# A decoder layer on one core: key weights' low halves in two pieces, half the last weight load behind two gathers, and expert tile 0 ahead of the last rows

## The chip, the cores and the metric

One Trainium2 chip, one core. The metric is the device time of one execution in microseconds (us); the median of several executions is compared.

## What is computed

`x` is 16 sequences of 128 tokens with 256 channels; `ctx` has the same shape. Cut to what matters, the reference is:

```
x = x + softmax(causal(rope(LN(x) Wq) . rope(LN(x) Wk) / 16)) (LN(x) Wv)
q, k, v = LN(x) Wq' + bq, ctx Wk' + bk, ctx Wv' + bv        8 heads of 128
x = x + concat(softmax(q . k over a dilated window of 64) v) Wc^T + bc
t = LN(x);  logits = silu(t rw1 + rb1) rw2 + rb2             8 experts, the best 2 of each token
x = x + t + sum over the 2 experts  w_e * (silu(t ew1_e + eb1_e) ew2_e + eb2_e)
```

LN is a layer norm over the channels. Matrices are 256x256 for the first attention, 1024x256 for each projection of the second, 256x512 and 512x256 for each expert.

## The kernel before, in words

**Numbers in two halves.** A float32 operand is held as a float16 "high" part and a float16 "low" remainder, and a product is three matmuls (high.high, high.low, low.high; the helper `three`, L1507 to L1512). ScalarE (ACT) writes high parts, VectorE (DVE) the low parts with a two-source instruction (value times a scale, minus the high part).

**Stages.** The 16 sequences go in four groups of 4 (512 tokens). For each group `front` does the first attention and the key and value projections of the second, `back` the queries, the window attention and the output projection. The first `front(0)` (called with r=None) also turns the weights into halves. `back(g)` and `front(g+1)` are in a hardware loop, the last ones stand outside it. After `back(3)` comes the expert stage: 39 tiles of 128 rows, 17 of which (`FULL`) can be filled from the first three groups; each tile is gathered from DRAM by an indirect DMA of GpSimd (POOL, `gather`), turned on TensorE (PE) (`turn`, L1680), copied by ACT (`take`, L744), put through its expert's two layers (`first_layer` L1868, `second_layer` L1882), weighted by DVE (`weigh_out`) and scattered. PE's loop over tiles (L1907) holds the second layer three tiles behind the first. The last group's layer norm, router and expert choice are done among the first tiles of that stage, in two halves of two sequences (`last_rows`, `last_turned`, `last_hidden`, `last_logits`, then `choose` and `weigh` on DVE).

**Order.** Each engine runs its own list in the order in which it is written; semaphores tie the lists together. There is no planner.

**The opening (`front(0)`).** On PE (L1581 to L1631): two products for rope's query halves, two for its key halves (all into the banks `pj0` and `pj1`), the values of the first attention into `ov` and `op`, then `project(g, 0, range(4))`, the first four of eight key products of the second attention, into `pj0` and `pj1` again; then the first attention's scores (L1611, L1616), which wait for both rope additions (`rope_add` 2) and for the masks (`ready` 2); then key products 4 to 7. Before the key products PE waits once for the key weights' low half (`w2_lo` 1, L1602). On DVE (L958 to L1000): the first rope pair (four multiplications, L967 and L968), then the context's low half (L822), the key weights' low half as one instruction of 128x2048 (L844), two casts (`identb` L975 and `masks` L976), then the second rope pair, which waits for POOL's first rope addition (`rope_add`, L963) because it overwrites `rope`; then the value weights' low half (L844 again). On POOL (L454 to L471 and L491 to L493): an addition and a subtraction for each rope pair (L461, L462), and ahead of the first a wait for the DMA that brings the bias row `bcs` (L492).

**Between `back(3)` and the tiles.** SP issues the load of all second-layer weights, four pieces of 1 MB one after the other (L413, L414), when the last scores are done. POOL: gathers 0 and 1, the last layer norm's power for half 0, gather 2, power for half 1, gather 3 and on (L519 to L530); gather 3 reuses the slot of tile 0, so it waits for ACT's `take(0)` and DVE's `take(0)` (which reads the tile's gate). ACT: high part of the last rows' half 0, `take(0)`, `take(1)`, `last_turned(0)`, and in the loop's first pass the high part of half 1, `take(2)`, `last_hidden(0)` (L766 to L783). DVE: low part of half 0, the residual of sequence 3, targets, a small low part, layer norm statistics of half 1, `last_turned(0)`, `take(0)`, `take(1)`, layer norm of half 1 (L1390 to L1437). PE: `turn(0)`, `turn(1)`, `last_rows(0)`, then tile 0's first layer, `turn(2)`, `last_hidden(0)`, tile 1's first layer (L1897 to L1941).

Of the kernel before, what the change touches and what calls it, by code (L numbers as in the profile page):

```python
# [16 lines left out]
P = 128  # L17
# [83 lines left out]
def decoder(nc, a, out):  # L101
# [9 lines left out]
    with ExitStack() as ctx:  # L111
# [221 lines left out]
        def _(sp):  # L333
# [77 lines left out]
            sp.wait_ge(sc_full[0], SC[0] * (G - 1) + 5)  # L411
            sp.wait_ge(sc_full[1], SC[1] * (G - 1) + 4)
            for i in range(4):  # L413
                sp.dma_start(down[:, 2 * i:2 * i + 2], split[:, 2 * i:2 * i + 2]).then_inc(split_in, 16)  # L414
            sp.wait_ge(b2_lo, 1)
            sp.dma_start(b2[E:2 * E, :], b2l[0:E, :]).then_inc(b2_lo_in, 16)
# [27 lines left out]
        def _(pool):  # L444
# [44 lines left out]
                            .then_inc(norm2, 1)  # L489

            power(1, 0)  # L491
            pool.wait_ge(bc_in, 16)  # L492
            front(0)  # L493
            with pool.Fori(0, G - 1) as g:
                back(g, True)
# [3 lines left out]
            def gather(t):  # L499
                s = t % SLOTS  # L500
                if t >= SLOTS:
                    pool.wait_ge(tp_free, t - SLOTS + 1)
                    pool.wait_ge(gated, t - SLOTS + 1)
                known = B if t >= FULL else OLD
                pool.indirect_dma_start(got[s], None, rows[0:known * L],  # L505
                                        bass.IndirectOffsetOnAxis(src_row[:, t:t + 1], 0),
                                        bounds_check=known * L - 1, oob_is_err=False).then_inc(gathered[s], 16)
# [14 lines left out]
            gather(1)  # L522
            power(3, G - 1, HALVES[0])
            gather(2)
            power(3, G, HALVES[1])
            for t in range(SLOTS, TILES):
                if t == FULL:
                    pool.wait_ge(row_out, 16 * G + 16)
                    pool.wait_ge(idx_done, 2)
                gather(t)  # L530
                if t >= TRAIL:
                    scatter(t - TRAIL)
                if t == CHOOSE + 5:
                    pool.wait_ge(gdiff, G)
                    pool.tensor_tensor(ge[:], euler[:], gd[:], ALU.pow).then_inc(gexp, 1)
                if t == NEW_LANES + 5:
                    pool.wait_ge(hot_t_done, 1)
                    pool.tensor_tensor(pay.rearrange("p (j t) -> p j t", j=JO + JN),
                                       hot_t.rearrange("p (j t) -> p j t", j=JO + JN),
                                       signed.unsqueeze(2).to_broadcast([P, JO + JN, REST]), ALU.mult).then_inc(pay_done, 1)  # L540
# [4 lines left out]
        def _(act):  # L545
# [183 lines left out]
            def last_high(h):  # L729
                high(3, G - 1 + h, row[:, HALVES[h], 0:D], HALVES[h])  # L730
# [33 lines left out]
                act.activation(hTh[t % SLOTS][:], hT[k][:], ACT.Copy, scale=MID).then_inc(h_hi, 1)  # L764

            act.wait_ge(row_out, 16 * (G - 1) + 16)  # L766
            last_high(0)
            take(0)
            take(1)
            last_turned(0)  # L770
            for t in range(TILES + 1):
# [20 lines left out]
        def _(dve):  # L792
# [46 lines left out]
                dve.wait_ge(tpB_full, TPB * g + 1)  # L839
                dve.tensor_copy(xTl[:], tpB[:].bitcast(F16)).then_inc(tpB_free, 1)  # L840

            def weights_low2(i, src):
                dve.wait_ge(w2_hi, i + 1)
                dve.scalar_tensor_tensor(out=w2l[:, :, 1024 * i:1024 * i + 1024], in0=src, scalar=UP,  # L844
                                         in1=w2h[:, :, 1024 * i:1024 * i + 1024], op0=ALU.mult,
                                         op1=ALU.subtract).then_inc(w2_lo, 1)

            def part_low(r, k):
                dve.wait_ge(part_hi, 4 * r + k + 1)
# [108 lines left out]
            def front(g, r=None, final=False):  # L958
                cosb = cosT.unsqueeze(1).to_broadcast([P, GB, P])
                sinb = sinT.unsqueeze(1).to_broadcast([P, GB, P])  # L960
                for i in range(2):
                    if r is not None or i:
                        dve.wait_ge(rope_add, 2 * g + i)  # L963
                    for half in range(2):
                        dve.wait_ge(pj_full[half], PJ * g + i + 1)
                        src = pj[half][:].rearrange("p (b t) -> p b t", b=GB)
                        dve.tensor_tensor(rope[:, 3 * half].rearrange("p (b t) -> p b t", b=GB), src, cosb, ALU.mult)  # L967
                        last = dve.tensor_tensor(rope[:, 1 + half].rearrange("p (b t) -> p b t", b=GB),  # L968
                                                 src, sinb, ALU.mult)
                        last.then_inc(pj_free[half], 1)  # L970
                    if i == 0:
                        if r is None:
                            context_low(0)
                            weights_low2(0, wkf)
                            dve.tensor_copy(identb[:], ident)  # L975
                            dve.tensor_copy(masks[:], cst[:, 2 * P:7 * P].rearrange("p (m k) -> p m k", m=5))\  # L976
                                .then_inc(ready, 1)
                        else:
                            norm(3, r, x2)
                if r is None:  # L980
                    weights_low2(1, wvf)
                else:
                    rows_low(r)
# [302 lines left out]
            def back(g, more):  # L1286
# [87 lines left out]
                if not more:  # L1374
                    sums(7)
                    transposed(6)
                    outputs_low(4)
                    sources(TABLE_OLD, FULL, 0)
                    outputs_low(5)
                    residual(1, op)  # L1380
                    transposed(7)
                    outputs_low(6)
                    tile_experts(full_first, full_n, FULL, 0)
                    outputs_low(7)
                    dve.wait_ge(op_free, OP * g + 2 + 2)
                    norm(3, G - 1, x2, HALVES[0])
                    residual(2, op)
                    pack(0, WORDS_FULL)
                    weights_low()
                    normed(3, G - 1, x2, HALVES[0])  # L1390
                    rows_low_half(0)
                    residual(3, sc1)
                    targets(FULL, 0)
                    dve.wait_ge(b2_hi, 1)
                    dve.scalar_tensor_tensor(out=b2l[0:E, :], in0=b2f[0:E, :], scalar=UP, in1=b2[0:E, :], op0=ALU.mult,
                                             op1=ALU.subtract).then_inc(b2_lo, 1)
# [35 lines left out]
            norm(3, G, x2, HALVES[1])  # L1432
            dve.sem_inc(y_free, 1)
            last_turned(0)
            take(0)
            take(1)
            normed(3, G, x2, HALVES[1])  # L1437
            for t in range(TILES + LAG + 1):
# [55 lines left out]
        def _(pe):  # L1494
# [86 lines left out]
            def front(g, r=None):  # L1581
# [31 lines left out]
                for b in range(GB):  # L1613
                    s = slice(b * P, (b + 1) * P)
                    for c in range(KC):
                        last = pe.matmul(sc0[:, s], qr[:, c, s], kr[:, c, s], start=False,  # L1616
                                         stop=(c == KC - 1), skip_group_check=True)
                last.then_inc(sc_full[0], 1)
                project(g, 0, range(4, 8))
                if r is not None:  # L1620
                    turn_rows(r, SC[0] * r + 6, SC[1] * r + 4)
# [4 lines left out]
                last.then_inc(tpA_full, 1)  # L1626
                if r is None:
                    pe.wait_ge(w2_hi, 2)
                    pe.wait_ge(w2_lo, 2)
                project(g, 1, range(1))  # L1630
                pe.wait_ge(tpA_free, TPA * g + 2)  # L1631
                for i, (bank_, full, free, use) in enumerate(first):
# [172 lines left out]
            pe.wait_ge(w1_lo, 1)  # L1805
            front(0)
            pe.wait_ge(w2_hi, 3)
            pe.wait_ge(w2_lo, 3)
            with pe.Fori(0, G - 1) as g:
                back(g, True)  # L1810
                front(g + 1, g)
# [88 lines left out]
            pe.wait_ge(packed_done, 1)  # L1900
            load(0)
            words = [experts()]
            last_rows(0)
            pe.wait_ge(up_lo, 1)
            pe.wait_ge(spare_lo, 3)
            pe.wait_ge(split_up_in, 16)
            for t in range(TILES + LAG):  # L1907
                k = column(t) % STEPS
                if t == 0:
                    pe.wait_ge(op_free, OP * G - 1)  # L1910
                if t == 1:
                    pe.wait_ge(op_free, OP * G)
                    pe.wait_ge(sc_free[1], SC[1] * (G - 1) + 4)
                if t < TILES:
                    first_layer(t, words[-1][k])
                then = None
                if t + 1 < TILES:
                    if column(t + 1) % STEPS == 0:
                        words.append(experts())
                    then = words[-1][column(t + 1) % STEPS]  # L1920
                if t < LAG and then is not None:
                    for m in range(MC):
                        addresses(then, m)
                if t == LAG:
                    pe.wait_ge(split_in, 64)
                    pe.wait_ge(b2_lo_in, 16)
                if t >= LAG:
                    old = column(t - LAG)
                    second_layer(t - LAG, words[old // STEPS][old % STEPS], then)
                if k == LOAD_AT and column(t) // STEPS + 1 < WORDS and t < TILES:  # L1930
                    if column(t) // STEPS + 1 == WORDS_FULL:
                        pe.wait_ge(packed_done, 2)
                    load(column(t) // STEPS + 1)
                if t + 2 < TILES:
                    turn(t + 2)
                if t == 0:
                    last_hidden(0)
                if t == 1:
                    last_rows(1)
                if t == 2:  # L1940
                    last_hidden(1)  # L1941
                if t == 3:
                    last_logits()
                if t == NEW_COUNTS:
                    ranks(slice(OLD, B), 2, LOGITS)
                if t == NEW_LANES + 3:
                    table(JO + JN, REST, 2, JO // 8 + 1, RANK_NEW)
# [94 lines left out]
```

## Time and profile before

| what | value |
|---|---|
| median of 3 runs | 481.01 us (480.35 to 483.81) |
| the profiled execution's own time | 480.62 us |
| its span in the trace | 478.8 us |
| time around the span | 1.82 us |
| granted TensorE clock, mean over the span | 0.982 of full |

Times in the rows are counted from the span's start. Engines are PE (TensorE matmul), PEld (its weight load), DVE (VectorE), ACT (ScalarE), POOL (GpSimd), SPq (the queue of the engine that issues DMAs). A row of a timeline is a run of like instructions: start, time, engine, line, operation, what is written and read, how many, and in brackets how long the engine was idle before it and what ended that. Buffers that share memory carry the name of the memory: the key weights' halves are `up_f`, the rope operands `up`, the gathered tiles `cst`.

### The profile page before, as it was taken

The page shows a single profiled execution, that of the slowest core. Times are in us where ns is not written, and L with a number is a line of the kernel's source. Part 1 is how long each engine was busy: PE and PEld are TensorE (multiplying, and loading weights), DVE is VectorE, ACT ScalarE, POOL GpSimd, SP SyncE. Part 2 cuts the span into 40 slices and gives each one's busy share as a digit, 9 for nine tenths or more (in the row PEclk, how much of TensorE's full clock was granted, in tenths as well). Part 3 has the DMA queues.
Part 4 walks back from the last instruction along what each step waited for, and adds up shares of the span by engine and source line. Part 5 has one row for each costly group of instructions (what it writes and reads, how often), then busy time and mean ns, then how long its engine had stood idle before and what let it go on. Part 6 is the DMA issues. An engine that isn't in the chain of part 4 may idle for free.

```text
span 478.8 us, 12291 instructions
## 1 busy us (share of the span) xinstructions
PE 444.6 (93%) x4211; PEld 306.3 (64%) x4211; DVE 346.8 (72%) x859; ACT 276.6 (58%) x716; POOL 165.4 (35%) x168
## 2 busy tenths in 40 slices
PE   8799999999998999999999998888899999999980
PEld 3356468856457865546785644677776788888850
DVE  5945467786876778696679688897678885555577
ACT  4454657526547526555762665573676777777740
POOL 1230123050203213012405020234346777777640
PEclk9989999999999999999999999999899999999995
DMA  8901000134230041621003423618113248223566
GB/s 323 371 40 46 0 2 1 36 99 168 97 133 0 0 131 44 219 88 45 1 15 117 134 86 135 242 54 341 41 46 125 76 139 270 81 81 88 157 230 244
DMA packets 20412, 54.43 MB, mean 114 GB/s; under 512 B 3365, under 2 KB 9774, under 8 KB 19600
## 3 DMA queue, kind: packets, MB, share of 16 engines
q1 hardware_dynamic: 16336, 43.34, 25.5%
q0 software_dynamic: 3744, 9.47, 6.9%
q10 hardware_dynamic: 288, 1.05, 0.6%
q8 instruction: 25, 0.41, 0.4%
q14 instruction: 19, 0.16, 0.1%
HBM read 37.00 MB, written 17.76 MB: 114 GB/s over the span
## 4 chain that ended last, share of the span: by engine, by line
PE 69%; DVE 15%; issue 10%; ACT 2%; POOL 1%; DMA 1%; DVEq 1%; POOLq 0%; ACTq 0%; SPq 0%
PE pj L1511 11%; PE pair L1511 10%; PE op L1788 8%; PE pair L1888 3%; PE tpA L1888 3%; PE sc L1878 3%; PE pj L1878 3%; PE pj L1760 2%; PE op L1878 2%; PE pair L1878 2%; PE sc L1727 2%; PE sc L1687 2%; ACT p L704 2%; PE pair L1890 2%; PE tpA L1890 2%
## 5 line engine op out<-in xcount | busy, mean ns | idle before, releaser
L1511 PE MATMUL pj<-up,up_f 128*128 128x512 f16 x240 | 58.9, 382 | 6.0 <-DVE rope L968 3.5
L704 ACT ACTIVATE p<-sc,nm 128x128 f32<-128x128 f32 (+1 forms) x128 | 41.8, 344 | 33.6 <-DVE nm L1338 33.5
L1511 PE MATMUL pair<-up,up_f 128*128 128x512 f16 x240 | 59.7, 386 | 0.2 <-DVE down L1342 0.2
L505 POOL DMA_INDIRECT cst<-rows,src_row x39 | 48.8, 1251 | 20.4 <-issue 8.0
L516 POOL DMA_INDIRECT picked<-wch,dst_row x39 | 40.1, 1029 | 24.2 <-issue 9.0
L452 POOL TENSOR_TENSOR rstd<-veps,nhalf 128x4 f32<-128x4 f32 (+1 forms) x13 | 12.7, 974 | 103.3 <-DVE veps L804 103.0
L1511 PEld LDWEIGHTS pj<-up,up_f 128*128 128x128 f16 x240 | 22.6, 98 | 34.8 <-issue 3.9
L1511 PEld LDWEIGHTS pair<-up,up_f 128*128 128x128 f16 x240 | 23.5, 99 | 28.8 <-DVE rope L968 1.5
L1788 PE MATMUL op<-wch,outs 128*128 128x256 f16 x240 | 40.3, 273 | 0.0
L487 POOL TENSOR_TENSOR pn<-p,inv 128x256 f32<-128x256 f32 x32 | 18.9, 612 | 44.0 <-DVE inv L1292 44.0
L461 POOL TENSOR_TENSOR up<-rope 128x512 f32<-128x512 f32 x8 | 12.4, 1552 | 60.7 <-DVE rope L968 49.4
L1788 PE MATMUL op<-wcl,outs 128*128 128x256 f16 x120 | 32.7, 273 | 0.0
L546 ACT ACTIVATE up_f<-sc 128x512 f16<-128x512 f16 x39 | 23.2, 594 | 15.6 <-PE sc L1687 15.6
L1888 PE MATMUL tpA<-down,up_f 128*128 x80 | 27.4, 379 | 0.4 <-issue 0.2
L1338 DVE TENSOR_REDUCE nm<-sc 128x4 f32<-128x512 f32 (+1 forms) x32 | 17.8, 555 | 13.4 <-PE sc L1732 7.2
L1888 PE MATMUL pair<-down,up_f 128*128 x76 | 26.2, 379 | 0.9 <-DVE up_f L1260 0.7
L577 ACT ACTIVATE down<-pj,bias 128x512 f32<-128x512 f32 x24 | 16.4, 684 | 18.0 <-PE pj L1511 18.0
L704 ACT ACTIVATION_READ_ACCUMULATOR p<-sc,nm 128x1 f32 x128 | 26.7, 209 | 0.0
L1260 DVE SCALAR_TENSOR_TENSOR up_f<-up_f 128x512 f16<-128x512 f32 x39 | 26.6, 682 | 0.0
L764 ACT ACTIVATE up_f<-up_f 128x512 f16<-128x512 f32 x39 | 24.6, 630 | 1.2
L1788 PEld LDWEIGHTS op<-wch,outs 128*128 128x128 f16 x240 | 22.3, 98 | 3.2
L1511 PE MATMUL pair<-up_f,up 128*128 128x512 f16 x96 | 23.3, 379 | 0.0
(294 smaller groups left out, 1111.3 us busy)
## 6 DMA issues: line engine op xcount, KB each, us to landing
raws<-in_staged SPq DMA_DIRECT2D x12, 512.0 KB, 5.4
split<-halved SPq DMA_DIRECT2D x12, 512.0 KB, 4.0
down<-split SPq DMA_DIRECT2D x4, 1024.0 KB
rows<-row SPq DMA_DIRECT2D x4, 528.0 KB
small<-in_x SPq DMA_DIRECT2D x4, 512.0 KB, 3.7
up<-in_ctx SPq DMA_DIRECT2D x4, 512.0 KB, 4.8
v<-in_w SPq DMA_DIRECT2D x2, 1024.0 KB, 9.2
resid<-outs SPq DMA_DIRECT2D x4, 512.0 KB, 2.8
```

The lines of the kernel that those rows point to most:

```text
L487: pool.tensor_tensor(pn2[:, 0, k], p2[:, 0, k], inv2[:, 0, k].unsqueeze(2).to_broadcast([P, 2, P]), ALU.mult)\
L505: pool.indirect_dma_start(got[s], None, rows[0:known * L], bass.IndirectOffsetOnAxis(src_row[:, t:t + 1], 0), bounds_check=known * L - 1, ...
L516: pool.indirect_dma_start(picked, bass.IndirectOffsetOnAxis(dst_row[:, t:t + 1], 0), ys[s], None, bounds_check=2 * B * L - 1, oob_is_err=F ...
L546: copy = lambda out, in_, scale=1.0: act.activation(out, in_, ACT.Copy, scale=scale)
L704: last = act.activation((p2[:, 0], p2h)[s][:, i, :], logit(s)[:, i, :], ACT.Exp, bias=nm2[:, s, i:i + 1], scale=1.0, accum_out=sum2[:, s, ...
L764: act.activation(hTh[t % SLOTS][:], hT[k][:], ACT.Copy, scale=MID).then_inc(h_hi, 1)
L1260: dve.scalar_tensor_tensor(out=hTl[s][:], in0=hT[t % BANKS][:], scalar=MID, in1=hTh[s][:], op0=ALU.mult, op1=ALU.subtract).then_inc(h_lo, 1)
L1511: last = pe.matmul(out, w(c), v(c), start=(i == 0), stop=(i == len(terms) - 1))
L1788: last = pe.matmul(dst[:, 0:D], o[:, b % 2, h, :], w[:, h, :], start=(h == 0 and k == 0), stop=(h == H - 1 and k == 2))
L1878: ins = pe.matmul(h[:, m * P:(m + 1) * P], up_rows[:, bass.ds(block(e, m, c, w), P)], xt[t % SLOTS][:, x, :], start=(c == 0 and i == 0), s ...
L1888: pe.matmul(y[:], hTh[q][:, m, :], down_rows[:, bass.ds(at, 2 * D)], start=(m == 0), stop=False, skip_group_check=True)
L1890: pe.matmul(y[:, 0:D], hTl[q][:, m, :], down_rows[:, bass.ds(at, D)], start=False, stop=False, skip_group_check=True)
```

## The change

1. The key weights' low half is made by two DVE instructions of 128x1024. The first (columns 0 to 511, key products 0 to 3) stays between the rope pairs; the second, and behind it the two casts, go behind the second rope pair and ahead of the value weights. PE waits for the second piece ahead of key product 4 (`w2_lo` 2), and the later counts of that semaphore go up by one.
2. POOL's wait for the bias row's DMA ahead of the first rope addition is gone. (The bias row is still waited for by DVE at L1026, whose result POOL waits for.)
3. Pieces 2 and 3 of the last weight load are issued only when gather 0 and gather 1 have landed.
4. Gather 3 is issued ahead of the power of half 1.
5. `take(0)` goes ahead of `last_high(0)` on ACT, and on DVE from behind `last_turned(0)` to ahead of the residual of sequence 3. On PE `last_rows(0)` goes behind tile 0's first layer, and `last_hidden(0)` from behind `turn(2)` to behind tile 1's first layer.

```diff
 (SP)
             for i in range(4):
+                if i >= 2:
+                    sp.wait_ge(gathered[i - 2], 16)
                 sp.dma_start(down[:, 2 * i:2 * i + 2], split[:, 2 * i:2 * i + 2]).then_inc(split_in, 16)
 (POOL)
             power(1, 0)
-            pool.wait_ge(bc_in, 16)
             front(0)
...
             power(3, G - 1, HALVES[0])
             gather(2)
+            gather(SLOTS)
             power(3, G, HALVES[1])
-            for t in range(SLOTS, TILES):
+            for t in range(SLOTS + 1, TILES):
 (ACT)
+            take(0)
             last_high(0)
-            take(0)
             take(1)
 (DVE)
-            def weights_low2(i, src):
+            def weights_low2(i, src, cols=slice(0, 1024)):
...
                         if r is None:
                             context_low(0)
-                            weights_low2(0, wkf)
-                            dve.tensor_copy(identb[:], ident)
-                            dve.tensor_copy(masks[:], cst[:, 2 * P:7 * P].rearrange("p (m k) -> p m k", m=5))\
-                                .then_inc(ready, 1)
+                            weights_low2(0, wkf, slice(0, 512))
...
                 if r is None:
+                    weights_low2(0, wkf, slice(512, 1024))
+                    dve.tensor_copy(identb[:], ident)
+                    dve.tensor_copy(masks[:], cst[:, 2 * P:7 * P].rearrange("p (m k) -> p m k", m=5))\
+                        .then_inc(ready, 1)
                     weights_low2(1, wvf)
...
                     rows_low_half(0)
+                    take(0)
                     residual(3, sc1)
...
             last_turned(0)
-            take(0)
             take(1)
 (PE)
                 last.then_inc(sc_full[0], 1)
+                if r is None:
+                    pe.wait_ge(w2_lo, 2)
                 project(g, 0, range(4, 8))
...
-                    pe.wait_ge(w2_lo, 2)
+                    pe.wait_ge(w2_lo, 3)
...
-            pe.wait_ge(w2_lo, 3)
+            pe.wait_ge(w2_lo, 4)
...
-            last_rows(0)
             pe.wait_ge(up_lo, 1)
...
                     first_layer(t, words[-1][k])
+                if t == 0:
+                    last_rows(0)
+                if t == 1:
+                    last_hidden(0)
...
-                if t == 0:
-                    last_hidden(0)
```

## Rows read from the trace of the kernel before

**Rows 1.** The page: busy time of PE and the chain that ended last.

```profile
PE 444.6 (93%) x4211; PEld 306.3 (64%) x4211; DVE 346.8 (72%) x859; ACT 276.6 (58%) x716; POOL 165.4 (35%) x168
...
PE 69%; DVE 15%; issue 10%; ACT 2%; POOL 1%; DMA 1%; DVEq 1%; POOLq 0%; ACTq 0%; SPq 0%
```

**Rows 2.** Timeline of the opening, 16 to 31 us.

```profile
16.10 1.21 DVE L822 SCALAR_TENSOR_TENSOR up<-up 128x1024 f16<-128x1024 f32 x1
...
17.23 2.29 DVE L844 SCALAR_TENSOR_TENSOR up_f<-v,up_f 128x2048 f16<-128x2048 f32 x1
...
18.92 1.47 PE L1511 MATMUL op<-up_f,up 128*128 128x256 f16 x12
18.99 1.65 POOL L461 TENSOR_TENSOR up<-rope 128x512 f32<-128x512 f32 x1 [11.32 <-DMA bcs<-in_bc]
...
19.43 1.29 DVE L975 CAST identb<-dc 128x128 bf16<-128x128 f32 x1
...
20.60 1.26 POOL L462 TENSOR_TENSOR up<-rope 128x512 f32<-128x512 f32 x1
20.65 1.57 DVE L976 CAST masks<-cst 128x640 bf16<-128x640 f32 x1
...
22.13 0.68 DVE L967 TENSOR_TENSOR rope<-pj,cst 128x512 f32<-128x512 f32 x1
...
23.56 1.63 PE L1511 MATMUL pj<-up,up_f 128*128 128x512 f16 x6 [3.16 <-DVE rope L968]
...
24.53 2.28 DVE L844 SCALAR_TENSOR_TENSOR up_f<-v,up_f 128x2048 f16<-128x2048 f32 x1
...
24.75 3.18 POOL L461 TENSOR_TENSOR up<-rope 128x512 f32<-128x512 f32 x1 [2.89 <-DVE rope L968]
24.98 2.77 PE L1511 MATMUL pair<-up,up_f 128*128 128x512 f16 x6
...
29.12 1.46 PE L1511 MATMUL pair<-up,up_f 128*128 128x512 f16 x6
...
30.42 0.38 PE L1611 MATMUL sc<-masks,identb 128*128 128x512 bf16 x1
```

**Rows 3.** POOL's rope addition and DVE's norm in the next group, same timeline.

```profile
99.38 1.27 POOL L461 TENSOR_TENSOR up<-rope 128x512 f32<-128x512 f32 x1 [13.92 <-DVE rope L968]
...
104.59 3.36 DVE L811 TENSOR_SCALAR xn<-outs,mv,rstd_up 128x256 f32<-128x256 f32 x4
```

**Rows 4.** Busy time by stretch: us, PE, PEld, DVE, ACT, POOL busy, clock, DMA share, GB/s.

```profile
20.00:24.00 4.00, 0.84 (x7) 0.34 (x6) 4.00 (x6) 2.40 (x2) 1.86 (x2) 1.00 1.04 393
24.00:28.00 4.00, 4.00 (x13) 1.47 (x12) 2.80 (x3) 0.90 (x2) 3.25 (x2) 0.59 0.28 115
...
40.00:44.00 4.00, 4.00 (x20) 2.20 (x19) 3.27 (x11) 0.88 (x3) 0.00 (x0) 1.00 0.15 23
```

**Rows 5.** DMA issues: the output projection's weights, KB, us from issue to landing.

```profile
down<-in_wc SPq DMA_DIRECT2D x1, 1024.0 KB, 14.8
```

**Rows 6.** Busy time by stretch during the last weight load (columns as in rows 4).

```profile
326.00:328.00 2.00, 1.93 (x45) 1.65 (x44) 1.19 (x3) 1.16 (x3) 1.56 (x2) 1.00 1.00 422
```

**Rows 7.** Timeline from the first gather to the expert choice, 326 to 352 us.

```profile
326.14 1.26 POOL L505 DMA_INDIRECT cst<-rows,src_row  x1 [2.52 <-DVE src_row L1185]
...
333.69 0.41 PE L1687 MATMUL sc<-dc,cst 128*128 128x128 f32 x2 [0.83 <-issue]
...
335.19 0.69 DVE L818 TENSOR_TENSOR row<-xn,row 128x512 f16<-128x512 f32 x1 [1.11 <-ACT row L546]
...
337.30 2.19 PE L1878 MATMUL op<-up_f,up 128*128 128x128 f16 x24
...
339.49 0.15 DVE L1272 TENSOR_SCALAR gate<-cst 128x1 f32 x1 [0.66 <-issue]
...
341.30 0.63 ACT L546 ACTIVATE row<-xn 128x512 f16<-128x512 f32 x1 [3.59 <-DVE xn L811]
...
348.86 0.48 DVE L887 TENSOR_SCALAR rope<-ov,rb1s 128x256 f32<-128x256 f32 x1 [1.99 <-ACT rope L741]
...
351.85 0.32 DVE L917 STREAM_TRANSPOSE logits_t<-ov 128x128 f32<-128x128 f32 x1
```

**Rows 8.** Busy time by stretch between those two (columns as in rows 4).

```profile
341.30:348.80 7.50, 7.01 (x100) 6.47 (x98) 3.80 (x10) 7.44 (x20) 3.72 (x4) 1.00 0.23 64
```

More of the change, by code:

```diff
@@ L840, in turned @@
                 dve.tensor_copy(xTl[:], tpB[:].bitcast(F16)).then_inc(tpB_free, 1)
-            def weights_low2(i, src):
+            def weights_low2(i, src, cols=slice(0, 1024)):
+                at = slice(1024 * i + cols.start, 1024 * i + cols.stop)
                 dve.wait_ge(w2_hi, i + 1)
-                dve.scalar_tensor_tensor(out=w2l[:, :, 1024 * i:1024 * i + 1024], in0=src, scalar=UP,
-                                         in1=w2h[:, :, 1024 * i:1024 * i + 1024], op0=ALU.mult,
-                                         op1=ALU.subtract).then_inc(w2_lo, 1)
+                dve.scalar_tensor_tensor(out=w2l[:, :, at], in0=src[:, :, cols], scalar=UP, in1=w2h[:, :, at],
+                                         op0=ALU.mult, op1=ALU.subtract).then_inc(w2_lo, 1)
             def part_low(r, k):
```

## The prediction

> **What bounds the kernel now.** The page comes first: PE is busy for 93% of the span and holds 69% of the chain that ended last, DVE 15% [rows 1]. So nearly all of the kernel is PE's, and an edit pays only where PE waits, or where it runs at its lower clock. The change touches two such places, and I read the timeline of each. In the opening PE finishes the first attention's values at 20.39 us (18.92 + 1.47) and then stands idle until 23.56, put down to DVE's second rope pair [rows 2]. PE is busy for 0.84 of the 4 us from 20 to 24, and in the 4 us after that its granted clock is 0.59 on average, that is, for most of them the lower level of 1.2 GHz instead of 2.4 [rows 4]. In the second place, after the last output projection, PE is idle for 0.83 us before the first tile is turned, and tile 0's first layer takes 2.19 us; but from 341.3 to 348.8 ACT is busy for 7.44 of 7.50 us [rows 7, 8].
>
> **Opening: when the second rope pair starts.** One fact of these rows must be understood first: POOL and DVE keep each other out. POOL's rope addition takes 1.27 us undisturbed [rows 3], but 3.18 when it starts at 24.75 into DVE's weight instruction, which runs to 26.81; 26.81 + 1.12 is its end [rows 2]. The other way round, the cast of only 128x128 takes 1.29 us beside POOL's first addition, the masks' cast ends 0.36 us behind POOL's second, and four norm instructions take 3.36 us beside two additions [rows 2, 3]. So between 16.1 and 22.2 us these instructions of DVE and POOL are one queue, whose length is a sum. Before, that sum is: context 1.13 (17.23 - 16.10), weights to 19.52, first addition to 20.64, second to 21.86, masks 0.36, and the second rope pair starts at 22.13. The bias row's DMA, on which POOL waits until 18.99, costs less than it looks: DVE holds the weights instruction until 19.52 anyway.
>
> After: POOL may start at 16.2, when the first pair is done, and queues behind the context's instruction, which started first. The sum is 16.10 + 1.13 (context) + 1.13 (a piece of 128x1024, as large as the context's) + 1.22 + 1.26 (POOL's two) = 20.84, in whichever order they take turns. The rope pair starts at 20.9 instead of 22.13. PE's first key product began 1.43 us behind it (23.56 - 22.13, the half of the pair that frees its bank), so it begins at 22.33: **1.23 us gained**, and PE's gap shrinks from 3.2 to 1.9 us.
>
> **Opening: from there to the scores.** Before, the four key products and the wait to the scores took 30.42 - 23.56 = 6.86 us. At full clock a product is spaced 1.30 us (29.12 to 30.42), four are 5.2; the rest is the low clock (the second product's 2.77 against 1.46) [rows 2]. After, two things must be ready. PE: 22.33 + 5.2 = 27.53 if the clock stays up. DVE and POOL: the rope pair ends at 20.9 + 4 x 0.6 = 23.3; the second piece 1.13 to 24.45, POOL's additions 1.22 and 1.26 to 26.95, masks 0.36 to 27.3. The scores start at about 27.6 instead of 30.42: **2.8 us gained**, the 1.23 included. Here late next is PE itself, with the masks 0.3 us ahead of it; the casts moved are hidden only by that much. The value weights' low half then runs from 27.3 to 29.6, and the row maximum that DVE must do when the scores are done (2 us behind their start) at 29.6 is met without loss. The new wait for the second piece (24.45) is over long before key product 4 at 29.6; behind it on PE is everything, but it waits for nothing. Behind this point PE is busy without a gap (4.00 of 4.00 us in the stretch at 40) at full clock [rows 4], and the last of the large weights to be used has landed at 6.62 + 14.8 = 21.4 (its issue at 6.62) [rows 5], so a DMA is not what is late next, and the gain is carried on through the PE-bound groups.
>
> Bounds on the clock: between 0.59 as before, which leaves 22.33 + 6.86 = 29.19, 1.23 us gained, and full clock, 2.8 us. I take full clock, because the gap is 1.3 us shorter and PE is at work from 22.3. The Trainium skill, "TensorE: Matmul & The Clock Gate", Part 1, says that the default is the throttled state, that recent activity releases it, and that the watching is free-running, not tied to the kernel's start; by it the same 1.9 us gap can lose the clock in one execution and not in another, which no row here shows; the sum by it is either of these two.
>
> **The last weight load and the gathers.** The load moves 422 GB/s and fills the DMA engines [rows 6]; gather 0 is issued at 326.14 and its tile is turned only at 333.69, 0.83 us after PE could [rows 7]. After, two 1 MB pieces (2.5 us each at that rate) are through by about 327, gathers 0 and 1 land near 329 to 330.5, and pieces 2 and 3 follow to about 336. They are needed by the second layer of tile 0, near 349: 13 us of cover; if gather 0 landed as late as now, they would end near 340, still covered. On SP the b2 copy stands behind the new waits (it waits for DVE until 337 anyway), and the rows and residual of group 3. Cost 0, gain for PE 0.8 us. Gather 2 moves beside piece 3 and may land 1 us later, at 336.5; its tile is turned near 338.
>
> **PE's new order.** turn(0) at 332.9, turn(1) behind ACT's take(0) at 334.1, tile 0's first layer at 334.9 (337.30 before), at full clock 1.34 us, last_rows(0) to 337.0, about 1 us of address work, turn(2) at 338, tile 1's first layer to 339.5, last_hidden(0) to 340.8. PE is then 2.4 us ahead of before.
>
> **But who waits for that.** DVE's list from 335.19 on is a chain: low part, residual, targets, statistics, last_turned(0), two takes, norm of half 1, ending at 341.27, and ACT's high part of half 1 starts at 341.30 after 3.59 us idle [rows 7]. take(0) is only moved within it (0.66 us of register load and the 0.15 us gate; behind a longer instruction some 0.25 of it may be covered). turn(3) needs ACT's take(2), which stands behind that high part, so PE waits until about 342.4 with most of its lead. From 341.3 ACT is full to 348.8 [rows 8], its tanh then releases DVE at 348.86, and DVE's four steps, a take and hidden_low end at 351.66; the choice of experts starts at 351.85 [rows 7]. That path loses 0.25 us of takes and 0.15 us between hidden_low and the logits: **0.4 us gained**. Bounds: 0 (DVE's register load covered nowhere) and 2.4 (PE's whole lead). POOL's power for half 1 now stands behind gather 3, which waits for take(0) (336.6) and is issued by 337.7; the power is asked for at 338.5 to 339.1, so no cost, but this cover is only 1 us.
>
> **Sum.** 480.62 - 2.8 - 0.4 = 477.4 us against the profiled execution's own time. That one lies 0.39 below the median of 481.01, so medians would be 477.4 to 477.8; I say 477.5.
>
> **Rivals.**
> - The clock falls in the opening again: 480.62 - 1.23 - 0.4 = 479.0. For it: a gap of 1.9 us is still there, and clocks fell behind the 3.2 us gap. Against: PE works right behind it. Chance 0.22.
> - PE's lead counts in the expert stage: if DVE's and ACT's chain from 335 is shorter than I read (take(0) moved frees more, or POOL's earlier gathers do), up to 2.4 us: 480.62 - 2.8 - 2.4 = 475.4. For it: PE is busy 7.01 of 7.50 us in the same stretch [rows 8], nearly a bound itself. Against: ACT's 7.44. Chance 0.16.
> - Slower: gather 0 lands late, and now everything hangs on it: ACT's take(0) stands ahead of the last rows' high part, DVE's ahead of the residual, and SP's last two pieces behind it. Today it has landed by 333.69, 7.5 us after its issue; from about 333.8 on, each us later would be a us of the chain that ends at 341.3. It outweighs the opening's 2.8 from 336.6 on, 10.5 us after issue; at 338 it is 480.62 - 2.8 + 4.2 = 482.0. For it: today's 7.5 us is long. Against: those are explained by 4 MB ahead of it in full DMA engines, and 2 MB go. Chance 0.03.
> - The change does nothing at the opening (the pair waits for something else) and 0.4 in the expert stage: 480.2. Against: the queue's sum ends at 22.2 and the pair starts at 22.13, so nothing else is left for it to wait for [rows 2]. Chance 0.04.
>
> **From the cases to the numbers.** My forecast has 0.55. 1%, 4.8 us, is about what a measurement of this kernel tells from no change; the forecast lies at 0.7%. Faster by over 1%: the second rival's 0.16. Slower by over 1%: 0.02 for things unseen. Within: 0.82. The range reaches from 475.3 (second rival) to 479.6 (first rival with the median's 0.4 and a little).
>
> **What would show it.** In the changed profile: POOL's first addition starts at 16.2 and lasts over 2 us; the second rope pair starts at 20.9; the first key product at 22.3; scores at 27.6; clock 1.00 from 24 to 28; maximum of the scores 2.8 us earlier. In the expert stage relative to PE's end of the output projection: turn(0) without a gap, tile 0's first layer 2.4 us earlier, but ACT's high part of half 1 and the start of the choice only 0 to 0.5 us earlier, and PE idle for over 1 us ahead of turn(3). Wrong would be: a low clock at 24 to 28, the choice 1 us or more earlier, or scores that wait for the masks.

## The result, and the profile after

The changed kernel takes 477.82 us in the median of 8 executions (477.01 to 478.94), the kernel before 481.96 in 8 (480.35 to 483.81). The ratio is 0.9913, with a 95% interval of 0.9889 to 0.9937. The profiled executions are 480.62 and 477.78 us, their spans 478.8 and 475.9. So the time fell by 2.84 us between the two profiled executions (2.9 in their spans) and by 4.1 between the medians, and both numbers have to be explained.

The opening after, in the timeline (it answers to [rows 2]); lines have moved down by 2 to 5, so L824, L847, L463, L464, L981, L982 and L1614 are L822, L844, L461, L462, L975, L976 and L1611 of before:

```profile
16.33 1.22 DVE L824 SCALAR_TENSOR_TENSOR up<-up 128x1024 f16<-128x1024 f32 x1
...
16.56 2.11 POOL L463 TENSOR_TENSOR up<-rope 128x512 f32<-128x512 f32 x1 [8.93 <-DVE rope L970]
17.46 2.29 DVE L847 SCALAR_TENSOR_TENSOR up_f<-v,up_f 128x1024 f16<-128x1024 f32 x1
...
18.63 2.25 POOL L464 TENSOR_TENSOR up<-rope 128x512 f32<-128x512 f32 x1
...
20.91 0.69 DVE L969 TENSOR_TENSOR rope<-pj,cst 128x512 f32<-128x512 f32 x1 [1.16 <-POOL up L464]
...
22.35 1.46 PE L1514 MATMUL pj<-up,up_f 128*128 128x512 f16 x6 [1.72 <-DVE rope L970]
...
25.66 1.57 DVE L982 CAST masks<-cst 128x640 bf16<-128x640 f32 x1
...
27.16 2.28 DVE L847 SCALAR_TENSOR_TENSOR up_f<-v,up_f 128x2048 f16<-128x2048 f32 x1
27.52 0.38 PE L1614 MATMUL sc<-masks,identb 128*128 128x512 bf16 x1
```

Each of POOL's additions and the weights piece of half the size last 2.1 to 2.3 us, nearly twice what they take undisturbed (1.27 us for the addition in [rows 3], 1.22 for the piece in a later run): they take turns. The first addition ends at 18.67, the piece at 19.75, the second addition at 20.88, and the second rope pair starts at 20.91, 1.22 us earlier than before. The first key product starts 1.21 us earlier and the scores 2.90 us earlier. So 1.69 of the 2.90 us come behind the first key product. That the clock is worth all of the 1.69 does not follow; the experiments below put it at 1.2 us in the old order. Against [rows 4] it is 1.00 instead of 0.59 in the stretch from 24 to 28 us (columns as there):

```profile
20.00:24.00 4.00, 2.28 (x14) 1.12 (x13) 3.09 (x5) 2.56 (x3) 1.34 (x2) 1.00 1.03 391
24.00:28.00 4.00, 4.00 (x22) 2.01 (x20) 4.00 (x4) 2.18 (x4) 2.88 (x2) 1.00 0.25 102
```

The place around tile 0, after (it answers to [rows 7]; all times are 2.7 us earlier already when the last output projection ends, at 330.12 instead of 332.85):

```profile
327.66 0.79 SPq L416 DMA_DIRECT2D down<-split  x2
...
329.96 0.38 PE L1692 MATMUL sc<-dc,cst 128*128 128x128 f32 x2
...
332.58 2.57 PE L1883 MATMUL op<-up_f,up 128*128 128x128 f16 x24 [0.71 <-ACT up_f L548]
...
333.54 0.15 DVE L1275 TENSOR_SCALAR gate<-cst 128x1 f32 x1 [0.74 <-issue]
...
338.15 0.63 ACT L548 ACTIVATE row<-xn 128x512 f16<-128x512 f32 x1 [1.94 <-DVE xn L813]
...
339.62 0.84 ACT L743 ACTIVATE rope<-ov,rb1half 128x256 f32<-128x256 f32 x2 [0.35 <-PE ov L1514]
...
342.96 0.41 PE L1692 MATMUL sc<-dc,cst 128*128 128x128 f32 x2 [1.34 <-ACT up_f L548]
...
349.04 0.31 DVE L919 STREAM_TRANSPOSE logits_t<-ov 128x128 f32<-128x128 f32 x1
```

Piece 2 of the weight load is issued at 327.66 and piece 3 right behind it, within the 0.79 us of this row, so gather 0 had landed 4.3 us after its issue at 323.40, and gather 1 by 328.45. Tile 0 is turned without a gap, and its first layer starts 2.46 us behind the output projection instead of 4.45. Yet the choice of experts (the last row) starts 18.92 us behind it instead of 19.00. PE had the lead and lost most of it waiting for ACT, 1.34 us ahead of the turn of tile 4. Of the 2.90 us gained at the scores, 2.73 are left at the end of the last output projection, 2.81 at the choice and 2.9 at the end of the span.

### The profile page after: what moved, and what is told of

Its sections match the earlier page's. It is cut to its first block, busy times and chain, and to the rows that moved or that the text cites. A ratio compares the mean times of both kernels' runs of the same rounds, so it can differ in the third digit from the quotient of the medians.

```text
span 475.9 us, 12293 instructions
## 1 busy us (share of the span) xinstructions
PE 444.0 (93%) x4211; PEld 306.2 (64%) x4211; DVE 348.7 (73%) x860; ACT 277.1 (58%) x716; POOL 166.4 (35%) x168
## 4 chain that ended last, share of the span: by engine, by line
PE 71%; DVE 12%; issue 9%; ACT 3%; POOL 2%; DVEq 1%; ACTq 0%; POOLq 0%
PE pj L1514 12%; PE pair L1514 10%; PE op L1793 8%; PE pair L1893 3%; PE tpA L1893 3%; PE op L1883 3%; PE sc L1883 3%; PE pj L1883 3%; PE pj L1765 2%; PE pair L1883 2%; PE ov L1801 2%; PE sc L1732 2%; PE sc L1692 2%; ACT p L706 2%; PE tpA L1895 2%
## 5 line engine op out<-in xcount | busy, mean ns | idle before, releaser
L1514 PE MATMUL pair<-up,up_f 128*128 128x512 f16 x240 | 58.3, 379 | 0.2 <-DVE down L1345 0.2
L463 POOL TENSOR_TENSOR up<-rope 128x512 f32<-128x512 f32 x8 | 11.8, 1479 | 58.1 <-DVE rope L970 58.1
```

Source lines behind the costliest of these rows:

```text
L1514: last = pe.matmul(out, w(c), v(c), start=(i == 0), stop=(i == len(terms) - 1))
```

## The experiments

Twelve kernels ran, four to a chip. Since the place of an event against the span's start moves by about 1 us between executions (the first rope product starts at 11.96 to 13.05), I compare three distances within each profile: from the first rope product on PE to the scores, from the end of the last output projection to ACT's high part of half 1, and from that same end to the choice of experts. The last column says for how long the clock of the profiled execution was at its lower level around tile 0: short is about 3 us, long about 7. In the opening it fell only in the profile of the kernel before. The mark for the first distance is this row, of the kernel before:

```profile
12.10 1.46 PE L1511 MATMUL pj<-up,up_f 128*128 128x512 f16 x6
```

| kernel | first product to scores | projection to high part | projection to choice | ratio to before (95%) | low clock around tile 0 |
|---|---|---|---|---|---|
| before | 18.32 | 8.45 | 19.00 | 1 | short |
| changed | 15.18 | 8.03 | 18.92 | 0.9913 (0.9889 to 0.9937) | short |
| opening alone | 15.19 | 8.44 | 18.86 | 0.9917 (0.9888 to 0.9946) | short |
| tile 0's parts alone | 17.11 | 8.03 | 18.62 | 0.9975 (0.9956 to 0.9994) | not at all |
| changed, again | 15.19 | 8.03 | 18.88 | 0.9902 (0.9876 to 0.9929) | short |
| bias wait put back | 16.13 | 8.03 | 18.60 | 0.9928 (0.9901 to 0.9955) | not at all |
| bias wait taken away alone | 17.08 | 8.44 | 20.58 | 1.0000 (0.9979 to 1.0021) | long |
| before, PE kept at work | 17.12 | 8.44 | 19.59 | 0.9976 (0.9957 to 0.9995) | long |
| hidden layer back | 15.18 | 8.02 | 18.28 | 0.9903 (0.9870 to 0.9936) | short |
| norm early | 15.19 | 7.21 | 17.98 | 0.9877 (0.9848 to 0.9906) | short |
| old order, PE kept at work | 15.19 | 8.43 | 18.87 | 0.9910 (0.9883 to 0.9936) | not at all |
| norm early, PE kept at work | 15.19 | 7.20 | 17.44 | 0.9880 (0.9854 to 0.9907) | not at all |
| opening alone, again | 15.18 | 8.43 | 19.05 | 0.9914 (0.9885 to 0.9943) | short |
| changed, third time | 15.19 | 8.03 | 18.96 | 0.9903 (0.9874 to 0.9933) | short |

**The two halves, each alone.** The opening alone is the changed kernel with SP's, ACT's, DVE's and PE's lines around tile 0 and gather 3 as before; the other is the reverse.

> Parts 1 and 2 of the change alone (the opening). Theory (the opening carries nearly all): second rope pair at 20.9, scores at 27.5, 2.8 us less than the kernel before, ratio near 0.994; the expert stage as before, shifted. Rival (PE's lead in the expert stage carries half or more): 1.5 us less or under.

> Parts 3, 4 and 5 alone (the last weight load, gather 3, the order around tile 0). Theory: the opening as before; tile 0's first layer 2 us earlier against PE's end of the output projection, the choice of experts 0 to 0.4 us earlier; total 0 to 0.4 us less, ratio 0.999 to 1.000. Rival: 2 us less or more, ratio 0.996.

> The changed kernel itself, beside the other three on one chip: 3 to 4 us less than before; the sum of the two halves if they are independent (opening 2.8, expert stage 0.1 to 0.4).

Measured: 477.66 us (7 executions) for the opening alone, 480.95 (12) for tile 0's parts alone, 477.66 (6) for the changed kernel, 482.26 (18) for the one before. So the opening carries nearly all of it, as the theory said, but the size is 4.6 us and not the 2.8 expected (the interval, 2.6 to 5.4 us, holds both). Tile 0's parts alone took 1.3 us off the median (interval 0.3 to 2.1), more than the 0 to 0.4 expected and less than the rival's 2. The halves do not add up as expected: 4.6 and 1.3 us alone, 4.6 together, where 3 to 4 had been expected. On the profile of tile 0's parts alone something else could be seen. In this execution the clock did not fall in the opening although nothing was changed there, and the scores then waited for POOL's last addition:

```profile
24.00:28.00 4.00, 4.00 (x20) 1.77 (x19) 2.73 (x2) 1.81 (x3) 3.32 (x2) 1.00 0.26 105
```

```profile
29.14 0.39 PE L1614 MATMUL sc<-masks,identb 128*128 128x512 bf16 x1 [0.32 <-POOL up L464]
```

That gives the first distance without a fallen clock, 17.11, and splits the opening's 3.13: 1.21 for the clock in the old order, 1.92 for the order with the clock up. What a fallen clock would cost in the new opening no run shows, since it never fell there.

The same profile shows a price that the staggered weight load has. Gather 2 is issued at 330.71, when pieces 2 and 3 of the load have just gone out (a DMA share of 0.93 from 330 to 332 us and of 1.01 in the 2 us behind), and PE waits for its rows ahead of the turn of tile 2, 6.9 us after that issue:

```profile
337.64 0.41 PE L1690 MATMUL sc<-dc,cst 128*128 128x128 f32 x2 [0.95 <-DMA cst<-rows,src_row]
```

In the changed kernel this gather takes as long (from 329.30 until PE's weight load at 336.19), with only 0.22 us of idle time of PE in front of the turn. The choice of experts is not later for it, at 18.62 us in the profile with PE's wait of 0.95.

**The bias row's wait, put back and taken away alone.**

```diff
 (put back, in the changed kernel)
+            pool.wait_ge(bc_in, 16)
             front(0)
```

```diff
 (taken away alone, in the kernel before)
-            pool.wait_ge(bc_in, 16)
             front(0)
```

> The changed kernel with POOL's wait for the bias row's DMA put back. Theory (DVE and POOL take turns): the first addition starts at 19.0 and is not held up, since DVE has nothing left, the second ends at 21.5, the second rope pair starts at 21.6 instead of 20.9, scores at 28.2: 0.65 us more than the changed kernel if the clock stays up; 1.3 more on top if it falls in the longer gap of PE. Rival (the wait costs what POOL shows as idle): 2.4 us more.

> The kernel before without POOL's wait for the bias row, nothing else. Theory (DVE and POOL take turns, only the sum of their work between the pairs counts): POOL starts at 16.2 but the second rope pair starts at 22.1 as before (16.1 + 1.13 + 2.29 + 1.22 + 1.26 + 0.36 = 22.4), gain 0 to 0.3 us. Rival (POOL's idle time was the cost): rope pair at 20.8 or earlier, 1.2 us less or more.

Put back, the first distance grows by 0.94 (expected 0.65), and the median was 478.59 against 477.66 beside it. POOL's two additions then run undisturbed:

```profile
18.96 1.27 POOL L463 TENSOR_TENSOR up<-rope 128x512 f32<-128x512 f32 x1 [11.43 <-DMA bcs<-in_bc]
20.19 1.26 POOL L464 TENSOR_TENSOR up<-rope 128x512 f32<-128x512 f32 x1
21.48 0.69 DVE L970 TENSOR_TENSOR rope<-pj,cst 128x512 f32<-128x512 f32 x1 [3.17 <-POOL up L464]
```

Taken away alone it brings nothing: POOL starts 2.7 us earlier, and the second rope pair starts at 22.12, against 22.13 in [rows 2]; the ratio is 1.0000. The same work is only queued in another order:

```profile
16.32 2.11 POOL L461 TENSOR_TENSOR up<-rope 128x512 f32<-128x512 f32 x1 [8.70 <-DVE rope L967]
17.23 3.35 DVE L843 SCALAR_TENSOR_TENSOR up_f<-v,up_f 128x2048 f16<-128x2048 f32 x1
...
18.40 3.31 POOL L462 TENSOR_TENSOR up<-rope 128x512 f32<-128x512 f32 x1
...
20.51 1.28 DVE L974 CAST identb<-dc 128x128 bf16<-128x128 f32 x1
21.72 0.48 DVE L975 CAST masks<-cst 128x640 bf16<-128x640 f32 x1
22.12 0.68 DVE L966 TENSOR_TENSOR rope<-pj,cst 128x512 f32<-128x512 f32 x1
```

So the wait was not the cost, and the rival that reads POOL's 11.32 us of idle time as one falls. It is worth 0.94 us only once the weights are in two pieces and the casts are out of the way. This profile also shows what a long fall of the clock can cost: its opening kept the clock, but around tile 0 the clock was at its lower level for about 7 us (twice as long as in the profile of before), and ACT's first tanh waited 1.22 us for the router's hidden layer on PE (in the changed kernel 0.35):

```profile
336.00:338.00 2.00, 2.00 (x23) 1.92 (x22) 1.63 (x7) 0.49 (x1) 0.48 (x1) 0.60 0.01 2
338.00:340.00 2.00, 1.24 (x9) 0.90 (x8) 0.88 (x5) 0.00 (x0) 0.78 (x2) 0.50 0.00 0
340.00:342.00 2.00, 2.00 (x12) 1.43 (x10) 1.09 (x3) 1.11 (x2) 1.54 (x2) 0.50 0.28 76
```

```profile
342.61 0.84 ACT L740 ACTIVATE rope<-ov,rb1half 128x256 f32<-128x256 f32 x2 [1.22 <-PE ov L1510]
```

Its choice of experts starts 20.58 us behind the projection, 1.58 later than in the profile of before, with the same order of work.

**PE kept at work in the old opening.**

```diff
+                    keep_warm(sc1, 14)
                     pe.wait_ge(w2_hi, 1)
```

> The kernel before with 14 matmuls of zeros into an idle bank in PE's gap of the opening. Theory (more than half of the opening's gain is the clock that no longer falls): clock 1.00 from 24 to 28 in every execution, key products at 1.30 us each, scores at 29.15 to 29.3 and then held by POOL's last addition, 1.2 us less than an execution of before in which the clock fell, and none of the high times of before. Rival (the gap alone counts): scores at 30.4 as before.

Measured: 481.08 us against 482.38, ratio 0.9976. The first distance is 17.12, just what the undisturbed opening showed, and the scores again wait for POOL's last addition (0.31 us). So the clock is worth 1.2 of the opening's 3.1 us, where the theory gave it more than half. That the matmuls of zeros are what held the clock in this profile is not shown: two profiles without them, those of tile 0's parts alone and of the bias wait taken away alone, kept it over gaps of 3.16 and 3.14 us. The median speaks for them (interval 0.2 to 2.1 us). The last part of the expectation failed: the executions still reach 482.8, and the profile has the clock low around tile 0 for some 7 us as well, with a distance of 19.59 there. The opening's clock is one thing, tile 0's another.

**Around tile 0: the hidden layer back, the norm early.** In the first, `last_hidden(0)` stands behind `turn(2)` again. In the second also, on DVE:

```diff
                     residual(3, sc1)
+                    dve.wait_ge(op_free, OP * (g + 1))
+                    norm(3, G, x2, HALVES[1])
                     targets(FULL, 0)
+                    last_turned(0)
+                    normed(3, G, x2, HALVES[1])
                     dve.wait_ge(b2_hi, 1)
...
-            norm(3, G, x2, HALVES[1])
             dve.sem_inc(y_free, 1)
-            last_turned(0)
             take(1)
-            normed(3, G, x2, HALVES[1])
```

> The changed kernel with the router's hidden layer of half 0 ahead of tile 1's first layer again, everything else changed. In the changed kernel ACT's first tanh waits 0.35 us for it, since tile 1's first layer stands ahead. Theory: no wait of ACT for PE there, the choice of experts 0.3 us earlier against PE's end of the output projection, total 0.3 us less or even. Rival: PE's order there doesn't matter, choice at the same distance.

> As the run before, and on DVE the norm of half 1 goes ahead of the targets, the small low part and the second take. Theory (DVE's and ACT's chain from the last residual sets the choice of experts): ACT's high part of half 1 starts 0.8 us earlier against PE's end of the output projection than in the changed kernel, the choice 0.8 to 1.1 us earlier, total 0.8 to 1.1 us less than the changed kernel. Rival (PE is the bound there): choice at most 0.3 earlier.

Measured: 476.86 and 476.26 us. In both ACT's first tanh no longer waits for PE. The choice stands 18.28 and 17.98 us behind the projection, 0.64 and 0.94 less than in the changed kernel, and the high part of half 1 in the second 0.82 earlier:

```profile
337.60 0.63 ACT L548 ACTIVATE row<-xn 128x512 f16<-128x512 f32 x1 [1.25 <-DVE xn L813]
338.77 0.84 ACT L743 ACTIVATE rope<-ov,rb1half 128x256 f32<-128x256 f32 x2
```

So DVE's and ACT's chain does set the choice, provided that PE's hidden layer is out of ACT's way; the changed kernel had put it in its way, which costs it something when the clock falls: in the two profiles with the changed order and no fall around tile 0 (tile 0's parts alone, bias wait put back) ACT waits for no hidden layer, and the choice stands at 18.62 and 18.60. Neither of the two kernels ran beside the changed one. Against the kernel before, the first has a ratio of 0.9903, which is that of the changed kernel (0.9902 to 0.9913), so its gain in the distance is not seen in the time; the second has the best ratio of this study, 0.9877, with an interval that reaches over the others.

**PE kept at work around tile 0, and both marks once more.**

```diff
 (4 and 7 in the old order; 0, 4 and 3 with the norm early, which also has 7 in the opening's gap)
+            pe.wait_ge(ov_free, TABLE_OLD)
+            keep_warm(ov, 4)
             turn(0)
+            keep_warm(ov, 7)
             turn(1)
```

> The opening's parts with the old order around tile 0, and 4 + 7 matmuls of zeros around the turn of tile 0. Theory (what the new order adds in the median is that it stands a fallen clock): the clock stays at 1.00 there, the distance from the end of the output projection to the choice of experts is 18.6 us instead of 18.9 to 20.6, the median 0.5 to 1 us below the opening alone and at the changed kernel's. Rival (the new order saves work of PE itself): distance 19 or more, median no better than the opening alone.

> The kernel with the norm of half 1 early, with 7 matmuls of zeros in the opening's gap and 4 + 3 around tile 0's turns. Theory: clock 1.00 in both places in every execution, distance to the choice 17.7 instead of 18.0, median 0.3 us below the same kernel without them (476.3) and 1 to 1.5 us below the changed kernel on this chip. Rival (the filler delays PE's own work): no better than 476.3.

> The opening's parts alone, once more, beside the changed kernel on the same chip: theory says 0 to 1 us above the changed kernel, with single executions 2 to 3 us above its best where the clock falls for long around tile 0. Rival: no difference in median or spread.

> The changed kernel once more, as the mark for the other three: 477 to 478 us, its executions within 2 us of each other.

Measured on one chip: 478.31, 476.50, 478.46 and 477.75 us, before 483.16. The clock did stay up in both filled kernels, 1.00 in every stretch around tile 0. In the old order that brought the distance only to 18.87, not to 18.6, and the median is that of the opening alone: against a short fall of the clock the filler buys nothing (19.05 in the profile of the opening alone beside it). So the expectation failed, and the rival's reading, that the new order also saves a little by itself, is nearer. The changed kernel's median is 0.7 us below that of the opening alone, within what was expected, but its executions spread over 2.8 us instead of the 2 expected, and those of the opening alone over 2.0. The longest of all four kernels is one of the changed kernel, 479.73 us, so long executions are not a mark of the old order. With the norm early the distance fell to 17.44 (expected 17.7), the median to 1.25 us below the changed kernel beside it, as expected; against the same kernel unfilled it can't be told (476.3 on another chip).

## Why the prediction was right, and what it missed

**The two halves, step by step.** These were forecast to the tenth: the second rope pair at 20.9 (20.91) and the first key product at 22.33 (22.35), by adding up what DVE and POOL do between the pairs; and the scores at 27.6 (27.52), with PE itself late next and the masks 0.3 us ahead of it. The start was 0.24 us later in this execution (first rope product at 12.34 instead of 12.10), so measured from there the sum was 0.24 us too cautious: the three turns took 1.12, 1.08 and 1.13 us. The clock was 1.00 from 24 to 28, the end of the bounds that I took. The experiments bear out the sum, but not the split in its bounds: with the clock fallen I had left the change 1.23 us, and so priced the clock at 1.6. In the old order it is worth 1.21, because with the clock up the scores still wait for POOL's last addition, which ends at 29.15; the order is worth 1.92.

**The expert stage.** PE's lead was forecast at 2.4 us and its uselessness too. Tile 0's first layer came 2.0 us earlier against the projection's end, the high part of half 1 0.42 us earlier (forecast 0.25), the choice 0.08 (forecast 0.4). Two steps of that were off. I put the end of PE's hidden layer at 340.8 and thereby ahead of ACT, at "full clock 1.34 us" for tile 0's first layer; it took 2.57 us with the clock falling, and even at 1.00 it takes 2.21 (tile 0's parts alone) and 2.10 (norm early, filled), where the first layer of tile 2 takes 1.50. Tile 0's is the only one whose weight addresses are not worked out ahead of it, which is the likely reason; no run took it away. Then ACT waited 0.35 us for PE. And I expected PE to stand ahead of the turn of tile 3; it stood ahead of that of tile 4. Gather 2 was put 1 us late at most, with its tile turned near 338; against the projection's end the turn came about 1 us later than that.

**The size in the medians.** The sum, 480.62 - 3.2 = 477.4, was made against a profiled execution, and that was one of the shorter ones: the first median of three was 481.01, that of eight 481.96, of the later sets 482.3 to 483.2. So the forecast of 477.5 came close to 477.82, but the gain between the medians, 4.1 us, is larger than the 3.5 forecast. Between the two profiles it is 2.84 against 3.2. The interval of the ratio reaches from 3.0 to 5.4 us, so 3.2 and 4.1 are not clearly different by this measurement.

What the rest is, if it is more than noise, stays open. The clock seems to have a part in it: in the 18 executions beside the first four experiments, the six with a mean clock of 0.982 or more have a median of 481.2 us, the twelve below it 482.7. The changed kernel's eight have 0.987 to 0.989 and a spread of 1.9 us, against 3.5 for before. That mean is a coarse measure, since it also counts the end of the span, where the clock is low for 8 to 14 us in every profile. A long fall around tile 0 does cost the old order time (20.58 and 19.59 us to the choice against 18.86 to 19.05 with a short one), and I had priced it at nothing, as not on the path. But it is not what the change removed there: the opening alone keeps the old order around tile 0 and has the same median as the changed kernel beside it, 477.66, and tile 0's parts alone still have executions of 482.0 and 482.9 us at a mean clock of 0.978. In the profiles of the changed kernel the fall around tile 0 was short, so whether the new order would stand a long one is not shown either. Nor do the distances explain the 1.3 us that tile 0's parts alone took off the median, with 0.38 us less to the choice. And it is not shown why the fall is long in some executions, or absent in others: in the kernel before PE is idle there twice, for 0.8 and 1.6 us, and the profile gives no more.

**What was luck.** That the clock stays up in the new opening was taken from the shorter gap of PE. The runs agree, but do not show that the gap is the reason: all ten profiles with the new opening kept it (in nine of them nothing was done to hold it), and two of three with the old opening and its 3.2 us gap kept it as well. So the prediction's doubt, that the same gap can lose the clock in one execution and not in another, is borne out for the old gap. The profile that the sum started from happened to be one in which it fell. Had it stayed up there, as in the other two, the opening would have had 1.9 us to gain instead of 3.1.

**The rivals.** The measured 0.9% lies within the 1% that I had called no change, with its interval reaching past it. The clock falling again in the opening: it kept 1.00 in all ten profiles that have the new opening, among them the one where the gap was 2.66 us (bias wait put back) and one with matmuls of zeros in the gap (norm early, PE kept at work). PE's lead counting in full: the choice moved by 0.08, so it fell. The late gather 0 fell, with a landing 4.3 us after issue at the latest; gather 2 was the late one, without harm to the choice. "No effect" fell.

## What to carry to other kernels

Where two engines shut each other out, as DVE and POOL do here, an idle engine's wait can be no cost and an earlier start no gain; add up what both must do between two points, and shorten that sum by moving work that nobody needs there (half the weights, the casts) behind it. Look at the granted clock behind every idle stretch of TensorE, and take the base from several executions: the clock can fall in one execution and stay up in the next, and a single profile shows only one of the two. And where one engine is brought forward, look at which in-order neighbour it now makes wait: with one router step behind a tile's first layer the choice started 0.6 us later (18.92 against 18.28).

## What the runs showed that I had not expected

Around tile 0 the clock fell in all five profiles of the old order in which nothing was done against it there; in the sixth, with 4 + 7 matmuls of zeros into an idle bank, it did not. That is one profile; in the changed order and its two variants it stayed up in two profiles of seven without any. A cast of 128x128 (to float16 it takes 0.23 us undisturbed) lasts 1.28 to 1.29 us every time that POOL's addition is ahead of it, yet the addition behind it lasts its 1.26 us undelayed in the openings of before and after. The steady part of the expert stage, from the choice to the last sums, varied between 113.72 us (opening alone) and 115.15 (changed, third time), 1.4 us, which alone is half of what this change brings between the profiles; differences below 0.5 us between medians of six executions say nothing here.
